# The turn of h inside the next gate/up product of the routed tiles, and one 32-bit product in place of three rounded ones

## The reference

```
x = x + 0.5 * ffn(layernorm(x))
x = x + attention(layernorm(x))
x = x + 0.5 * ffn(layernorm(x))
```

## Time and profile before

| | us |
|---|---|
| median of 3 runs | 1179.36 (1179.07 to 1181.36) |
| the profiled execution, its own time | 1182.96 |
| its span, first to last instruction | 1181.3 |
| TensorE matmuls busy | 1116.7 (95%) |
| VectorE busy | 674.8 (57%) |
| ScalarE busy | 567.6 (48%) |
| GpSimd busy | 469.3 (40%) |

### The profile page before, as it was taken

The page is one execution under the profiler, slowest core; times in us unless marked ns, Lnnn a source line. Parts: engine busy times, 40 slices in busy tenths (PEclk is TensorE's granted clock), DMA queues, the critical chain, the costliest instruction groups (busy, mean ns, idle before and its releaser), DMA issues.

```text
span 1181.3 us, 20221 instructions
## 1 busy us (share of the span) xinstructions
PE 1116.7 (95%) x5982; PEld 931.3 (79%) x5983; DVE 674.8 (57%) x1826; ACT 567.6 (48%) x1512; POOL 469.3 (40%) x486
## 2 busy tenths in 40 slices
PE   5989997889999999999999999999999988989996
PEld 4867775778888888888888888888888876877774
DVE  6657768755444545455445454454544456667767
ACT  3346652356445536454545454544543543356640
POOL 1456548116315325323423532522531410455543
PEclk9999999899999999999999999999999999999999
DMA  9984556101101000010110110010100017744546
GB/s 355 388 335 165 171 173 221 54 1 37 54 2 36 35 19 5 31 53 0 36 53 0 36 53 0 36 53 0 36 1 1 1 36 272 310 146 162 171 155 190
DMA packets 38603, 114.61 MB, mean 97 GB/s; under 512 B 4384, under 2 KB 4384, under 8 KB 36512
## 3 DMA queue, kind: packets, MB, share of 16 engines
q1 hardware_dynamic: 33440, 97.30, 22.8%
q0 software_dynamic: 5120, 16.78, 4.2%
HBM read 79.20 MB, written 34.87 MB: 97 GB/s over the span
## 4 chain that ended last, share of the span: by engine, by line
PE 84%; DVE 5%; issue 3%; ACT 3%; DMA 3%; POOL 1%; SPq 0%; DVEq 0%; ACTq 0%; POOLq 0%
PE bank L1291 23%; PE bank L1360 15%; PE bank L1376 8%; PE bank L1326 8%; PE bank L1270 6%; PE bank L1196 6%; PE bank L1304 6%; PE bank L1278 3%; PE bank L1213 2%; PE bank L1239 2%; POOL x_rows L490 1%; PE bank L1372 1%; PE bank L1322 1%; DMA experts<-in_ffn_w 1%; DVE x L1015 1%
## 5 line engine op out<-in xcount | busy, mean ns | idle before, releaser
L517 POOL TENSOR_TENSOR scores<-scores,pinv 128x512 f32<-128x512 f32 (+3 forms) x256 | 176.4, 721 | 367.0 <-DVE pinv L1052 367.0
L467 POOL TENSOR_TENSOR tback_lo<-experts,tback_hi 128x768 fp32r<-128x768 f32 x62 | 114.2, 1844 | 77.9 <-ACT tback_hi L622 77.8
L708 ACT ACTIVATE scores<-scores,nmax 128x512 f32<-128x512 f32 (+3 forms) x256 | 140.3, 558 | 0.5 <-DVE nmax L1042 0.5
L682 ACT ACTIVATE pT_hi<-bank 128x512 fp32r<-128x512 f32 (+2 forms) x192 | 86.9, 487 | 108.0 <-PE bank L1304 108.0
L720 ACT ACTIVATE oT_hi<-bank 128x512 fp32r<-128x512 f32 x64 | 38.3, 598 | 208.7 <-PE bank L1372 208.7
L1022 DVE TENSOR_TENSOR pT_lo<-bank,pT_hi 128x512 fp32r<-128x512 f32 (+2 forms) x192 | 100.8, 553 | 48.4 <-ACT pT_hi L682 48.4
L1042 DVE CUSTOM_DVE_ANT_0 scores<-bank,causal 128x512 f32<-128x512 f32 (+3 forms) x256 | 112.2, 486 | 1.5 <-issue 0.5
L1360 PE MATMUL bank<-wds_hi,oT_hi 128*128 128x512 f32 x256 | 105.9, 414 | 1.4 <-DVE oT_lo L1026 1.4
L1291 PE MATMUL bank<-xnT_hi,wqs_hi 128*128 128x512 f32 x256 | 106.4, 416 | 0.1
L1026 DVE TENSOR_TENSOR oT_lo<-bank,oT_hi 128x512 fp32r<-128x512 f32 x64 | 44.2, 691 | 108.6 <-ACT oT_hi L720 108.6
L1291 PE MATMUL bank<-xnT_lo,wqs_hi 128*128 128x512 f32 x256 | 100.8, 394 | 0.0
(11 more groups left out here) (199 smaller groups left out, 2923.7 us busy)
## 6 DMA issues: line engine op xcount, KB each, us to landing
experts<-in_ffn_w SPq DMA_DIRECT2D x32, 768.0 KB, 11.0
xn<-x_rows SPq DMA_DIRECT2D x62, 256.0 KB, 2.7
y_rows<-xn SPq DMA_DIRECT2D x62, 256.0 KB, 2.0
raw_q<-in_wq SPq DMA_DIRECT2D x8, 1024.0 KB, 6.1
raw_d<-in_wd SPq DMA_DIRECT2D x8, 1024.0 KB, 4.9
x_rows<-experts SPq DMA_DIRECT2D x1, 7936.0 KB, 30.5
raw_w<-in_ffn_w SPq DMA_DIRECT2D x8, 768.0 KB, 6.0
raw_kv<-in_wkv SPq DMA_DIRECT2D x8, 512.0 KB, 3.3
```

The lines of the kernel that those rows point to most:

```text
L467: nc.gpsimd.tensor_tensor(tback[par][1][:], experts[:, bass.ds(at + FRONT, GU - FRONT)], tback[par][0][:].bitcast(F32), ALU.subtract).then ...
L517: nc.gpsimd.tensor_tensor(s, s, pinv[k % 2][:, i:i + 1].to_broadcast([P, P * (i + 1)]), ALU.mult).then_inc(att.normed, 1)
L682: nc.scalar.activation(pT[0][:, lo_col:hi_col], bank[b][:, 0:hi_col - lo_col], ACT.Copy).then_inc(att.t_hi, 1)
L708: nc.scalar.activation(s, s, ACT.Exp, bias=nmax[par][:, i:i + 1], scale=-1.0, accum_out=psumr[par][:, i:i + 1]).then_inc(att.exp, 1)
```

## The change

- All 32 steps are written out, with no loop. The word with the expert numbers is read at the end of every fourth step (on ACT ahead of the silu), so that all counts that are waited for are constants.
- The last of the four chunks of gate/up is one plain 32-bit matmul (two records) of 256 columns, on an unsplit `x_last` and the expert's own weights. It stands first in the group, ahead of the wait for the front. `xT` then holds three chunks, `tback` 512 columns, and ACT copies the fourth chunk of x by itself.
- The turn of h of tile j-1 moves into gate/up of tile j, behind its second group: last chunk, first chunk, turn of h, chunks two and three. The down product stays where it was.
- On ACT the two copies of x move ahead of hT.
- The waits for the shared part's additions at the first tiles are split over the first two turns of h and down products. Pads keep the other tiles at their addresses.

```diff
-        def tile_steps(eng, step, loads=False):
-
-            at, there = places(eng, 0, loads)
-            for k in range(4):
-                step(0, k, at, there)
-            with eng.Fori(1, TILES // 4) as it:
-                at, there = places(eng, it, loads)
-                for k in range(4):
-                    step(it, k, at, there)
-            at, there = places(eng, TILES // 4, loads)
-            for k in range(TILES % 4 + 1):
-                step(TILES // 4, k, at, there)
+        def tile_steps(step):
+
+            for j in range(TILES + 1):
+                step(j // RING, j % RING)
+
+        def next_word(it, k):
+
+            return k == RING - 1 and it < TILES // RING
...
                 def turned(par, count):
                     act.wait_ge(m.x_mm, count)
-                    nc.scalar.activation(xT[par][0][:].rearrange("p c t -> p (c t)"), bank[2 + par][:],
-                                         ACT.Copy).then_inc(m.x_out, 1)
+                    nc.scalar.activation(xT[par][0][:].rearrange("p c t -> p (c t)"), bank[2 + par][:, 0:3 * P], ACT.Copy)
+                    nc.scalar.activation(x_last[par][:], bank[2 + par][:, 3 * P:], ACT.Copy).then_inc(m.x_out, 1)
...
-                    nc.scalar.activation(tback[par][0][:], experts[:, bass.ds(at + FRONT, GU - FRONT)],
+                    nc.scalar.activation(tback[par][0][:], experts[:, bass.ds(at + FRONT, GU - 2 * FRONT)],
                                          ACT.Copy).then_inc(tile_part.back_hi, 1)
...
                         back(1 - par, at[k + 2], there[k + 2])
-                    if exists(j, 1, TILES):
+                    if j <= TILES - 2:
+                        turned(1 - par, j + 2)
+                    if j >= 1:
                         act.wait_ge(m.h_mm, j)
                         nc.scalar.activation(hT[:], bank[4 + 1 - par][:, 0:P],
                                              ACT.Copy).then_inc(m.h_out, 1)
-                    if exists(j, 0, TILES - 2):
-                        turned(1 - par, j + 2)
+                    if j <= TILES - 2:
 
                         act.wait_ge(tile_part.front_mm, base + j + 1)
                         front(at[k + 2])
+                    if next_word(it, k):
+                        at, there = places(act, it + 1, loads=True)
...
+                def turn_hidden(j, par):
+                    pe.wait_ge(m.mul, j)
+                    if isinstance(j, int) and j <= 2:
+
+                        pe.wait_ge(ffn[n].added, HALF * (BEFORE - 1) + j)
+                    wait(pe, m.h_out, j - 1)
+                    nc.tensor.transpose(bank[4 + 1 - par][:, 0:P], ht[:], ident[:]).then_inc(m.h_mm, 1)
...
                         pe.wait_ge(tile_part.x_lo, base + j + 1)
+                        wait(pe, m.mul, j - 1)
+                        into = bank[par][:, 0:2 * INTER]
+                        nc.tensor.matmul(into, x_last[par][:], experts[:, bass.ds(at[k + 1] + 3 * FRONT, FRONT)],
+                                         start=True, stop=False)
                         pe.wait_ge(tile_part.front_lo, base + j + 1)
-                        wait(pe, m.mul, j - 1)
-                        i = 0
-                        for c in range(HC):
+                        for c in range(HC - 1):
                             if c == 1:
                                 last.then_inc(tile_part.front_mm, 1)
+                                if j >= 1:
+                                    turn_hidden(j, par)
                                 pe.wait_ge(tile_part.back_lo, base + j + 1)
```

More of the change, by code:

```diff
@@ L122, in build @@
             with ExitStack() as sub:
-                xT = [pair("xT0", [P, HC, P], sub)]
+                xT = [pair("xT0", [P, HC - 1, P], sub)]
+                x_last = [sb("x_last0", [P, P], F32, sub)]
+                sb("front_pad", [P, P], F32, sub)
                 tfront = pair("tfront", [P, FRONT], sub)
                 sb("held", [P, 4 * HID], F32, sub)
-                tback = [None, pair("tback1", [P, GU - FRONT], sub)]
-                xT.append(pair("xT1", [P, HC, P], sub))
-                tback[0] = pair("tback0", [P, GU - FRONT], sub)
+                tback = [None, pair("tback1", [P, GU - 2 * FRONT], sub)]
+                sb("back_pad", [P, 2 * FRONT], F32, sub)
+                xT.append(pair("xT1", [P, HC - 1, P], sub))
+                x_last.append(sb("x_last1", [P, P], F32, sub))
+                sb("turn_pad", [P, P], F32, sub)
+                tback[0] = pair("tback0", [P, GU - 2 * FRONT], sub)
                 hT = sb("hT", [P, P], F32, sub)
@@ L466, in back, with step @@
                     pool.wait_ge(tile_part.back_hi, base + count)
-                    nc.gpsimd.tensor_tensor(tback[par][1][:], experts[:, bass.ds(at + FRONT, GU - FRONT)],
+                    nc.gpsimd.tensor_tensor(tback[par][1][:], experts[:, bass.ds(at + FRONT, GU - 2 * FRONT)],
                                             tback[par][0][:].bitcast(F32),
                                             ALU.subtract).then_inc(tile_part.back_lo, 1)
-                def step(it, k, at, there):
+                def step(it, k):
+                    nonlocal at
                     j, par = 4 * it + k, k % 2
-                    if exists(j, 0, TILES - 2):
+                    if j <= TILES - 2:
                         back(1 - par, at[k + 2], j + 2)
+                    if next_word(it, k):
+                        at, _ = places(pool, it + 1)
                 pool.wait_ge(route[n].table, 1)
-                back(0, places(pool, 0)[0][1], 1)
+                at, _ = places(pool, 0)
+                back(0, at[1], 1)
                 low_dn(n, BEFORE // 2)
-                tile_steps(pool, step)
+                tile_steps(step)
             def feed_forward(n):
@@ L652, in routed @@
                 cut_dn(n, BEFORE // 2)
-                tile_steps(act, step, loads=True)
+                tile_steps(step)
             def high_part(hi, lo, raw, count):
@@ L994, in step @@
                         nc.vector.tensor_copy(xn[:, RING + (k - 1) % 4, :], bank[6 + 1 - par][:]).then_inc(m.y_out, 1)
+                    if next_word(it, k):
+                        at, _ = places(dve, it + 1)
                 dve.wait_ge(route[n].table, 1)
-                at = places(dve, 0)[0]
+                at, _ = places(dve, 0)
                 front(at[1], 1)
@@ L1002, in routed @@
                 dve.wait_ge(route[n].scattered, 2 * TT * 16)
-                tile_steps(dve, step)
+                tile_steps(step)
             def combine(n, t):
@@ L1269, in step @@
                             for a, b in PARTS:
[L1270 to L1273, removed]
+                                last = nc.tensor.matmul(into, xT[par][a][:, c, :], piece[b][:, start:start + FRONT],
+                                                        start=False, stop=(c == HC - 2 and (a, b) == PARTS[-1]))
                         last.then_inc(m.gu_mm, 1)
@@ L1276, in step @@
                         pe.wait_ge(m.h_out, j)
+                        if isinstance(j, int) and j <= 2:
+                            pe.wait_ge(ffn[n].added, HALF * (BEFORE - 1) + 2 + j)
                         wait(pe, m.y_out, j - 2)
@@ L1280, in step @@
                         last.then_inc(m.y_mm, 1)
-                tile_steps(pe, step)
+                    if next_word(it, k):
+                        at, _ = places(pe, it + 1)
+                at, _ = places(pe, 0)
+                tile_steps(step)
             def attention():
```

18 lines of the change are left out of this document (8 added, 10 removed).

## The result

| | before | after |
|---|---|---|
| median of 4 runs, us | 1179.82 (1179.07 to 1181.36) | 1170.66 (1168.59 to 1172.93) |
| ratio, 95% interval | | 0.9923 (0.9901 to 0.9944) |
| the profiled execution's own time, its span | 1182.96, 1181.3 | 1171.64, 1169.9 |
| TensorE busy | 1116.7 (95%) | 1114.2 (95%) |
| ScalarE, GpSimd busy | 567.6, 469.3 | 567.4, 436.1 |

Faster by 9 us, 0.8%. The forecast was 1181.2 with a range from 1173.5; the result lies outside it. The two profiled executions differ by 11.4 in span and not by 9: that of before stood 3.1 above the median of this table, that of after 1.0.

What follows compares the result with a forecast made beforehand. TensorE was taken as the bound, with one hiccup per loop turn and ScalarE close behind. Steps of 3.13 us plus word reads gave +1.0 in the first FFN and +0.8 in the second: 1181.2 against 1179.36, range 1173.5 to 1187.7.

Steps and rivals of the forecast that it cites:

- TensorE's pieces: Each routed step on TensorE: three rounded products (0.36) go, one 32-bit product (0.43) comes, net +0.07 us; 2.92 without waits.
- Copy of hT: On ScalarE: starts 0.31 us after the turn of h, takes 0.28; the copies of x ahead leave 0.12 of cover.
- The weight load 0.33 after the copy ends: On TensorE before the down product: hT loads as weights 0.33 us after its copy, two address operations in between.
- (d): Rival, down product: address operations run ahead of the wait, no stall for hT, steps of 2.92, 10.5 off, 1170.7; chance 0.12.
- H + 1.04: Down product starts 1.04 us after the turn of h starts (H); TensorE is free at 0.83, so each step stalls 0.2.
- b = 0.2: TensorE's word read behind the down product: 0.2 us lost for each of seven reads a stage, bounds 0 and 0.5.
- The head of the first FFN: Down product there starts at 92.58 as before, since a weight load from memory ends at 87.30 whatever the change does.
- The head of the second FFN: First down product moves from 1049.30 to about 1048.5, given back at 1065.76 where a tile's x arrives late.
- The jump: Loop turn on TensorE: writing out removes a jump of 0.21 us, seen 12 times; a possible saved fetch was left out.
- (a): Rival, TensorE's sequencer behind the down product: word read in full, 0.5 lost each, +3.6 us on the forecast, 1184.8; chance 0.24.
- (b): Rival, ScalarE becomes the bound: hT behind the two copies of x, those 0.25 late, +6.5 us, 1187.7; chance 0.13.
- (c): Rival, routed stages: a cheaper step of 3.05 and a word read loss near 0.1, 5.2 us off, 1176.0; chance 0.16.

Runs made afterwards that it cites:

- the early address: Changed kernel, but TensorE computes the down product's address and reads the next word ahead of the wait for hT: 1185.78 us, 0.9891 of the kernel before.

## Why the prediction was wrong, step by step

- **What bounds the kernel**: right in the main. TensorE's own 2.84, and some 0.3 of waiting, most of it from ScalarE's late start at the loop's head. The prediction gave one wait of 0.61 in four steps as the source of four times 0.3. The steps of before are 2.84, 3.08, 2.94, 3.78: the long one is 0.94 over, and two others hold 0.3. Written out alone, the steps are 2.89.
- **TensorE's pieces**: right. New product 0.43, net +0.07, a step without waits 2.92 (measured 2.92 in the changed kernel, 2.91 with the early address).
- **Copy of hT**: right, 0.31 after the turn, 0.28 long. ScalarE's cover held: it stands idle for 0.24 ahead of the copy of hT, where 0.12 of cover was forecast. VectorE's low part of the front was mostly short, as forecast: 0.43 in the median where it was 0.82.
- **The weight load 0.33 after the copy ends**: the step that failed. It was 0.14. The prediction took the 0.33 of the earlier trace rows with its two register operations over into the new kernel, and set rival (d) aside with the words "and the code order is unchanged". The order of the down product's code is unchanged, but not what it has to compute. The new product uses `at[k + 1]` one step before the down product uses the same value, and the records fit that its result is kept: two plain operations for each of the 62 new products, and 14 for the 62 down products. What stood behind the wait in before (two operations and the final addition) shrank to the addition. The kernel with the address decoded twice brought back both the late load, 0.38, and the long steps, 3.16. The term was H + 1.04 and measured H + 0.83, and over 50 steps that is the 10.5 that (d) priced, with another cause than (d) gave: no operation of the down product moved ahead of the wait, two were done for another instruction.
- **The word read, b = 0.2**: about right. The step with it is mostly 3.1 for 2.92, once 3.26, twice 2.92, and the first tile of the new word adds 0.09 (its one plain operation left behind the wait), which the prediction did not have. In the kernels without the 32-bit product the reads cost next to nothing.
- **The head of the first FFN** "equal at 92.58": it was 91.24. The expert at 87.30 was no longer what came last. The chain there is the load of a tile's x, 8.90 us from 80.17 (the chain has a copy of y and the issue of its store ahead of it), then the turn at 89.11:

```profile
80.17 8.90 DMA xn<-x_rows
```

- **The head of the second FFN** "gained and given back": it was gained in part. The late x is there again,

```profile
1065.74 4.27 DMA xn<-x_rows
```

  but for a later tile, and the stage still came out 4.1 shorter. The head itself brought 1.2 where 0.8 was forecast.
- **The sum**: from tile 4 to the last down product of the first FFN 80.9 was forecast, 76.2 measured (91.24 to 167.43). The failed step stands in all 26 steps, 5.5 of that (the last two measured 2.48 and 1.64 where 2.69 and 1.90 were forecast). Six first tiles of a word at 0.09 take 0.5 back, and a late x at 107.2, which the prediction did not foresee, takes 0.4. The word reads came to 1.0 instead of 1.2. That leaves the 4.7. The forecast of +1.8 less 50 x 0.21 is -8.7, and the medians show -9.2. That this comes so near, and that (d) with 1170.7 names the median itself, is luck in part: the heads, 1.3 in the first FFN and 0.4 more than forecast in the second, and the 1.1 outside the routed stages stand in no term of it, and the two profiled executions differ by 11.4.
- **The jump**: the prediction read 0.21 us, 12 times, on TensorE. That is what its record shows, but not what the loop costs. Jump and loop arithmetic together cost 0.35 in four steps where ScalarE is the one that is late (12.63 less 12.28), and jump, read and addresses cost TensorE 0.9 at the head of a loop turn when the change stands in the old loop, where it no longer waits for another engine. The Trainium skill ("Runtime: NRT & Kernel Launch", Instruction fetch mechanics) says that a taken branch out of the window must fetch first, which could be a part of this; no run here parts a fetch from the arithmetic beside it.
- **Rivals**: (a), (b) and (c) did not occur. The signs listed for the forecast came out so: no wait of the turn of h for VectorE, ScalarE's gap gone, steps longer at the word: seen. Even steps of 3.13 and a wait for hT in each: not seen, which was named as the sign of (d).

What the prediction did not weigh at all is how the gain splits. It treated the change as one thing whose parts offset each other. The parts in four steps, from 12.63: writing out -1.05, the hidden turn with the new order on ScalarE -0.2 (11.58 to 11.39), the 32-bit product +0.25 by its own length (to 11.64, with the early address), and the word reads and register work that show with it +0.4 (to 12.03). The 32-bit product gives back half of what the rest brings.

## What to carry to other kernels

Before a latency is carried over from a row to a changed kernel, list the instructions inside it and ask of each whether the change still needs it there: register operations for an address count, and another use of the same value one step earlier removes them. Work out addresses and read index words ahead of the wait, not behind it: on TensorE 0.4 us in four steps was gained so without leaving anything out of the computation, and on ScalarE 0.7 us by where the word is read. When a change has several parts, price each alone: here the 32-bit product, which makes the cuts on ScalarE and GpSimd shorter (GpSimd's busy time fell by 33 us, ScalarE's did not fall), cost time, since neither was the bound once the steps were written out.

## What was not expected of the hardware

- Two more register operations behind a wait, 36 ns each by their records, moved the weight load of the last tile from 0.14 to 0.33 behind the copy's end. With the final one at 94 ns in place of 51 as well, it was 0.37 there and 0.38 in the loop. The records make up 0.08 of the first difference of 0.19; on ScalarE's chain above such operations stand with some 0.03 of issue between them.
- TensorE's read of a word from SBUF into a register took 0.56 us in the median in the changed kernel, where it stands behind the down product, and 0.30 where it stood ahead of the wait for hT. The place in the code is not the reason by itself: in the kernel that is only written out the read also stands behind the down product, and its median was 0.30. On ScalarE the read had a median of 0.29 in the changed kernel, and 0.44 at the head of the step in the kernel that reads there.
- A plain 32-bit product of 256 columns costs TensorE 0.43, that is 0.22 a record, against 0.36 for three rounded products. In two kernels it cost 0.48 to 0.49: where it followed the turn of h directly, and, behind the turn of x, where ScalarE copied hT ahead of x.
